# A ring of five steps instead of four for the gathered rows of a graph network kernel

## The reference

```python
# layer 0: messages along edges
e = edge_feats @ W_e + b_e
m = relu(e + node_feats[src])
agg = segment_sum(m, dst)
h = agg + (1 + eps) * node_feats
z = relu(batchnorm(h @ W1 + b1)) @ W2 + b2
x = layernorm(x + z)
# layer 1: three graph convolutions
for W, b in ((W0, b0), (W1, b1), (W2, b2)):
    h = relu(segment_sum((h @ W)[src] * norm, dst) + b)
x = layernorm(x + h)
```

## Time and profile before

| what | value |
|---|---|
| median of 3 runs | 3328.69 us (3327.97 to 3330.57) |
| the profiled execution's own time | 3303.86 us |
| its span, first to last instruction | 3301.8 us |
| DVE busy | 2422.1 us, 73% |
| PE busy | 2546.6 us, 77% |
| POOL busy | 1553.7 us, 47% |
| granted TensorE clock, mean | 0.844 |

### The profile page before, as it was taken

The page is one execution under the profiler, slowest core; times in us unless marked ns, Lnnn a source line. Parts: engine busy times, 40 slices in busy tenths (PEclk is TensorE's granted clock), DMA queues, the critical chain, the costliest instruction groups (busy, mean ns, idle before and its releaser), DMA issues.

```text
span 3301.8 us, 43418 instructions
## 1 busy us (share of the span) xinstructions
PE 2546.6 (77%) x13276; PEld 2023.7 (61%) x13276; DVE 2422.1 (73%) x4250; ACT 1587.7 (48%) x2907; POOL 1553.7 (47%) x1687
## 2 busy tenths in 40 slices
PE   4676777767676776766666777667799999999998
PEld 3555555555555555555555555555578888888887
DVE  6887887777777777777777777778778984445554
ACT  3544544444444444444444444445655555445444
POOL 6676666666666666666666666665200000000111
PEclk7777777777777777778777777778899999999999
DMA  5334333333333333333333333333233333333342
GB/s 179 109 111 151 109 113 111 111 111 110 111 111 110 110 110 111 111 112 111 111 111 113 111 110 111 113 108 105 90 125 153 130 119 148 124 130 151 149 175 81
DMA packets 157585, 394.57 MB, mean 120 GB/s; under 512 B 36944, under 2 KB 100587, under 8 KB 151979
## 3 DMA queue, kind: packets, MB, share of 16 engines
q1 hardware_dynamic: 104620, 278.06, 22.5%
q0 software_dynamic: 51008, 105.74, 14.1%
q10 hardware_dynamic: 1728, 7.92, 0.6%
HBM read 286.78 MB, written 104.80 MB: 119 GB/s over the span
## 4 chain that ended last, share of the span: by engine, by line
DVE 40%; PE 30%; another core or an unknown queue 16%; issue 8%; ACT 4%; DMA 1%; DVEq 0%; SPq 0%; ACTq 0%; POOL 0%; POOLq 0%
DVE z L1323 17%; PE psE L1156 13%; PE psA L1156 12%; DVE work L1305 5%; DVE held L1317 5%; DVE work L1330 5%; DVE work L1331 4%; DVE onehot L1311 3%; PE psE L445 2%; ACT z L863 1%; DMA work<-in_edge_cols 1%; PE psA L1027 1%; PE psA L1096 1%; ACT z L855 1%
## 5 line engine op out<-in xcount | busy, mean ns | idle before, releaser
L785 POOL DMA_INDIRECT work<-in_x_flat,idx x1563 | 1496.8, 958 | 795.4 <-issue 422.5
L855 ACT ACTIVATE z<-psA 128x490 int32 x392 | 223.9, 571 | 1207.6 <-PE psA L1027 859.5
L1323 DVE TENSOR_SCALAR z<-iota_r,key,scale 128x490 bf16<-128x490 f16 x1568 | 716.0, 519 | 3.1 <-issue 2.6
L445 PE MATMUL psE<-we,work 128*128 128x256 f32 x1564 | 662.3, 568 | 6.9 <-issue 4.7
L442 PE MATMUL psE<-edge_bias,ones_b 128*128 128x512 bf16 x391 | 221.7, 567 | 488.9 <-DMA work<-in_edge_cols 336.9
L445 PEld LDWEIGHTS psE<-we,work 128*128 128x128 f32 x1564 | 465.8, 298 | 151.5 <-issue 63.0
L1011 PE MATMUL psS<-onehot,work 128*128 128x72 f32 x3126 | 419.0, 286 | 125.6 <-issue 71.2
L1011 PEld LDWEIGHTS psS<-onehot,work 128*128 128x128 f32 x3126 | 394.1, 202 | 167.4 <-issue 159.5
L1027 PE MATMUL psA<-z 128*128 128x245 bf16 x3136 | 447.0, 292 | 60.0 <-issue 58.3
L863 ACT ACTIVATE z<-iota_c,low 128x128 bf16<-128x128 f16 x1568 | 476.8, 389 | 0.0
L1156 PE MATMUL psE<-wide,halves 128*128 128x500 f32 (+1 forms) x2058 | 448.6, 375 | 5.8 <-ACT halves L957 5.4
(11 more groups left out here) (176 smaller groups left out, 2236.7 us busy)
## 6 DMA issues: line engine op xcount, KB each, us to landing
counts<-adjacency SPq DMA_DIRECT2D x36, 3062.5 KB, 9.8
adjacency<-work SPq DMA_DIRECT2D x392, 245.0 KB
work<-in_edge_cols SPq DMA_DIRECT2D x196, 256.0 KB
work<-in_x_flat,idx POOLq DMA_INDIRECT x1563
counts<-adjacency SPq DMA_DIRECT2D x3, 1592.5 KB, 6.2
acc<-in_x_cols ACTq DMA_DIRECT2D x1, 3136.0 KB
xn<-in_x_rows SPq DMA_DIRECT2D x1, 3136.0 KB
x_spill<-xn SPq DMA_DIRECT2D x12, 256.0 KB, 2.2
```

The costliest lines, as they stand in the source:

```text
L445: mm = pe.matmul(psE0[0:n, 2 * q:2 * q + 2, :].rearrange("p j f -> p (j f)"), eaT[:, slot, q, 0:n], we[:, :], start=False, stop=True, skip ...
L785: gp.indirect_dma_start(gath[:, g % R, j, :], None, x_flat[:, :], bass.IndirectOffsetOnAxis(ap=idx[:, g, j:j + 1], axis=0)).then_inc(rows_ ...
L855: act.activation(taken[:, w % TAKEN, :, :], ring[:, bass.ds(at, 2 * HC)].rearrange("p (a n) -> p a n", a=ODD), ACT.Copy).then_inc(evac_ok, 1)
L1323: ve.tensor_scalar(hot[:, k % RB, :], iota_r[:, :, 0:2 * HC // ODD], key[:, k:k + 1], scale[:, k:k + 1], ALU.is_equal, ALU.mult).then_inc( ...
```

## The change

The ring of gathered rows gets a fifth slot. The slot takes floats 4096 to 5119 of `work`, where the edge features were; these move up into the 1024 floats that nothing used, and `full` stays where it was (5120 + 1024 = 6144). POOL's wait for `win_mm` begins at step 5 and asks for the window product of step g - 5; there are five semaphores `rows_in` instead of four. The steps' gathers, their indices and every other instruction are the same, and the indices of the first 20 steps still come by a DMA of their own.

```diff
--- before.py
+++ after.py
@@ -18,7 +18,7 @@
 J = 8
 GE = P * J
 W = 72
-R = 4
+R = 5
 D = 20
 DP = D // 4
 HP = 4
@@ -167,7 +167,7 @@
         zf = z[:, :, :].rearrange("p a n -> p (a n)")
 
         gath = work[:, 0:R * J * F].rearrange("p (r j f) -> p r j f", r=R, j=J)
-        eaT = work[:, 4096:4096 + RE * HP * P].rearrange("p (r j e) -> p r j e", r=RE, j=HP)
+        eaT = work[:, R * J * F:R * J * F + RE * HP * P].rearrange("p (r j e) -> p r j e", r=RE, j=HP)
         onehot_at = here()
         onehot = sb("onehot", [P, 2, J, W])
         held = sb("held", [P, 2, W])
@@ -188,7 +188,7 @@
 
         hot = zf[:, 0:RB * HC].bitcast(BF16).rearrange("p (r n) -> p r n", r=RB)
         lows = zf[:, RB * HC:RB * HC + LB * J * P // 2].bitcast(BF16).rearrange("p (s q n) -> p s q n", s=LB, q=J)
-        full_at = 4096 + RE * J * P
+        full_at = R * J * F + RE * HP * P
         full = work[:, full_at:full_at + SLOTS * 2 * HC].bitcast(U16).rearrange("p (s b h n) -> p s b h n", s=SLOTS, b=2, h=2)
         taken_at = RB * HC + LB * J * P // 2
         taken_row = 2 * HC // ODD
```

## The result

The kernel with five slots took 3337.87 us (median of 10 runs, 3336.13 to 3340.34), the kernel before in the same session 3329.09 us (10 runs, 3327.36 to 3330.80). The ratio is 1.0027, 95% interval 1.0019 to 1.0035: slower by 8.8 us (6.3 to 11.7). The prediction said 3328.2 us, within 3322 to 3336, and no measurable change.

What follows compares the result with a forecast made beforehand. The prediction took a loop from DVE over SP's store and the edge load to PE and back as the bound, with POOL off it. All terms were 0 except 0.5 us gained at the end: 3328.69 - 0.5 = 3328.2 us, range 3322 to 3336.

Steps and rivals of the forecast that it cites:

- Work of POOL: POOL's gathers over the program: the same 1563, 938 ns at least and 944 in the middle, none added.
- Steady steps: Main loop: POOL always catches up, so its bursts start at the same moments, one step number ahead; 0 us.
- The prediction's own last sign: Main loop's end: moving by more than 7 us without any rival's signs would mean a missed mechanism.
- The start: First steps: POOL's 5.74 us wait goes, gain 0; one burst moved ahead costs 0 to 7.0 us, taken 0.
- rival B: Between 48 and 89 us: the burst moved ahead delays edge loads beside it; 7.0 us slower, 3335.7 us; chance 0.05.
- The end: Last steps: gathers finish one period earlier, one more edge load runs without traffic; gain 0 to 1.2 us, taken 0.5.
- Moved edge features: Edge features at their new place, with SP's load: same sizes and same waits, no address effect; 0 us.
- Waits at line 1305 stay: DVE before line 1305: the nine waits, 45.4 us, come from late PE and not late rows, so they stay.
- The lead: Gathered rows before DVE's additions: they lie there 8 to 12 us before DVE asks, taking 3.4 or 7.1 us to land.
- Rival A: DVE at line 1305: rows are late and the fifth slot removes those waits; 18 us faster, 3310 us; chance 0.07.
- Rival C: Steady loop: POOL's silence shifts against the edge load; 3312 or 3344 us; chance 0.05 faster, 0.03 slower.

Runs made afterwards that it cites:

- before: The kernel before, unchanged, in the execution profiled for the prediction: 3303.86 us.
- c0_before: The kernel before, unedited, profiled a second time for comparison with the changed kernel: 3326.05 us, ratio 1.0001.
- f3_re4: The kernel before with four slots for the edge features instead of two, so they load two steps earlier: 3327.26 us, ratio 0.9994.
- f2_half: The kernel before with only half of each step's gathers made from step 4 on, leaving out gathered rows: 2795.73 us, one execution.
- e3_late4: The changed kernel with step 4's wait for the first window product put back, POOL ahead from step 5 on: 3337.05 us, ratio 1.0031.
- f1_ahead60: The changed kernel with POOL held to the old wait distance up to step 59 and the new one from step 60: 3340.15 us, ratio 1.0034.
- e2_edge_moved: The kernel before with only the edge features moved to their new place, four slots and waits as before: 3326.46 us, ratio 0.9998.
- f5_r3: The kernel before with a ring of three slots for the gathered rows: 3327.49 us, ratio 0.9995.
- g2_chunk: The kernel before with POOL waiting after four of eight gathers for an earlier DVE signal, a 2.5 us pause: 3429.66 us, ratio 1.0311.
- g4_hot: The kernel before with POOL waiting after four of eight gathers for a DVE signal expected to be raised by then: 3335.86 us, ratio 1.0028.
- g1_held: The kernel before with POOL waiting after four of eight gathers for DVE's held_ok, pausing up to 9.4 us: 3755.14 us, ratio 1.128.

## Why the prediction was wrong, point by point

**Work of POOL, 0 us.** Right: 1563 gathers, 938 at the least and 946 ns in the middle.

**Steady steps, 0 us.** The number was right (2011.6 against 2010.9 us for 170 steps), the reason wrong, and this is the step that failed: "POOL hangs on this loop and isn't a link of it". The prediction had the clue in hand, a matmul recorded 9 us before three engines went on in one moment, and set it aside with "I can't say from the records why it is seen so late". It then read the loop by what lay nearest, the edge load. That POOL's 9.69 and 2.02 us make up the period of 11.72 says nothing, as busy and idle time of any engine do. What could have told it stood in two other rows. POOL's wait is 1.93 us on average over 179 steps and 2.01 and 2.02 us in the two of the earlier trace rows, each time about as long after its own last gather: a wait for PE would vary with PE. And the one wait that POOL began long before PE was ready ended 1.6 us behind PE's matmul (`before`: 52.25 and 53.88 us; 0.27 us in c0_before) and not 9, with PE named as the releaser and not "remote". f3_re4 took the edge load away and f2_half the half of the burst: the first changed nothing, the second took 491 us off those 170 steps. The prediction's own last sign came true as well: the last line 1335 moved from 2350.9 to 2361.5 us with none of the rivals' signs, which was to mean a missed mechanism.

**The start, gain 0, cost 0 to 7.0, taken 0 us.** Here the missed link is paid for. The prediction asked only whether the moved burst would slow the loads beside it. As the runs read, DVE's step s can't end before POOL has gathered as far ahead as the ring lets it, since only then does POOL fall silent. At this start it is DVE's signal `held_ok` that the fifth burst delays, by 7.95 us instead of 0.35, and PE's first product moves by 8.4 us. One slot more is one burst more ahead of every step: 8 gathers of 0.95 us and 8 gaps of 0.30, 10.0 us. Measured: 8.4 to 12.8 us up to step 20, 11.2 to 15.6 in e3_late4, 13.4 in f1_ahead60. One burst is thus the right size, but the price is mostly higher, and what adds to it isn't settled. It isn't a matter of the start, where rival B had put it: e3_late4 and f1_ahead60 pay it where POOL gets ahead.

**The end, gain 0 to 1.2, taken 0.5 us.** The right sign, too small. It isn't one quieter edge load. When the gathers are finished, DVE's steps run at their own 8.88 us and no longer at 11.8, and with five slots one more of them does: 2.9 us. The timeline of DVE at the end, changed kernel first, then c0_before:

```profile
2304.58 0.31 DVE L1335 TENSOR_TENSOR acc<-psS,acc 128x144 f32 x1 [2.89 <-remote]
2316.42 0.31 DVE L1335 TENSOR_TENSOR acc<-psS,acc 128x144 f32 x1 [2.87 <-remote]
2325.31 0.30 DVE L1335 TENSOR_TENSOR acc<-psS,acc 128x144 f32 x1
```

```profile
2302.94 0.31 DVE L1335 TENSOR_TENSOR acc<-psS,acc 128x144 f32 x1 [2.86 <-remote]
2314.72 0.31 DVE L1335 TENSOR_TENSOR acc<-psS,acc 128x144 f32 x1 [2.81 <-remote]
2323.60 0.30 DVE L1335 TENSOR_TENSOR acc<-psS,acc 128x144 f32 x1
```

Both have one step at 11.8 and the next at 8.9, but the changed kernel stands there one step number earlier. The sum of the two by one burst: +10.0 - 2.9 = +7.1 us, against +8.8 (6.3 to 11.7) measured.

**Moved edge features, 0 us.** Right: e2_edge_moved, ratio 0.9998.

**Waits at line 1305 stay.** They aren't there for the rows, as was argued: both kernels have them, 14.1 us in 3 waits after, 7.5 in 2 before, and the number changes from execution to execution. With three slots (f5_r3) the time is the same too. The lead was larger than the prediction took it: the trace has the packets of the gathers, and in c0_before the last packet of a burst ends 1.2 us after POOL's last gather (median), not 3.4 to 7.1. Rival A falls.

Among the rivals, B had the right sign and nearly the size (3335.7 us), but by luck, for a reason that the runs don't bear out: edge loads beside the early burst, where f3_re4 shows that edge loads are not the bound. Its own sign is missing too: between 40 and 90 us PE waits 0.9 us for edge features in the changed kernel and 1.9 us in c0_before. The Trainium skill's rule that queues take turns on a DMA engine (DMA: Bandwidth & Descriptors, section "Queues, rings and completion order"), quoted there against the change, is thus not what cost the time. Rival C didn't happen.

**Still open.** Why signals are held back by POOL's gathers, and by what part of them. In c0_before the last packet of a burst ends 1.2 us after POOL's last gather and the signal of the window product comes 0.6 us behind that, so the rows' traffic fits as well as POOL's issuing; f2_half and g2_chunk stop both at once, and no run separates them. Nor is it known which signals pass. Between 300 and 2280 us of c0_before the window product's signal came in mid burst once in 168 steps, but of the 334 count signals (line 1027, two a step) 176 did, 162 of them during the burst's second gather. So in almost every step one signal of PE, raised as the burst begins, comes through some 2 us later, and the next one, the window product's, raised some 2.7 us into it, stays out for 9 us. The Trainium skill says of TensorE (Perfetto Trace Analysis, section "Tensor Engine Instruction (MATMUL, LD_WEIGHTS)") that the end of a matmul in the profile is estimated, and that the signal is pushed once PSUM has acknowledged the last byte. The trace agrees that the recorded end isn't the signal's time (8.85 us apart in c0_before, 0.01 us in f2_half). Open too is the shorter period of the execution that the prediction read, 11.72 against 11.82 us.

## What to carry to other kernels

A deeper ring is free only if the engine that fills it is off the path. If its work is a link of the loop, each slot more puts one filling more ahead of every step, and at the end it gives back only the difference between the loop's period and that of the next-slowest engine. The filling shows in the time only where nothing else holds the start: from three slots to four it did not, from four to five it did. Where several engines go on in one moment, always the same time after another engine's burst, and long after the releaser is recorded, suspect the burst: look for the same wait at a place where that engine had been idle before, and cut the burst in half as a test before costing it at zero.

## What the runs showed of the hardware that was not expected

- A signal of PE is there 0.01 us after the recorded end of the matmul, and ends POOL's wait 0.27 us after it, when POOL has been silent for 3 us (f2_half, 1004.63 to 1004.90). While POOL issues indirect DMAs at a distance of 1.25 us, the window product's signal comes nearly always only when it stops: DVE's line 1335 or 1337 starts 1.9 to 3.2 us after the last gather's end. A gap of 0.50 us (g4_hot) was nearly never enough, one of 2.5 us (g2_chunk) was.
- It isn't PE's signals alone, and not all of them. At the start of the changed kernel DVE's `held_ok` is there 7.95 us after line 1317 (54.00 to 61.95 us), in c0_before 0.35 us after it; and half of PE's count signals come in mid burst (176 of 334, c0_before).
- In long runs of gathers PE's instructions come slowly: in g1_held PE stands 642.7 us before its line 1013 put down to "issue", 389 times. The timeline of PE there shows one matmul at a time where otherwise 16 run together:

```profile
1019.97 0.28 PE L1013 MATMUL psS<-onehot,work 128*128 128x72 f32 x1 [2.58 <-issue]
```

- Half the gathers are worth 491 us in 170 steps (2.89 us a step), although POOL is busy less than half of the program and DVE and PE three quarters of it.
